# Graph network on one core: nodes numbered 49p+w, first edges found in a resident list

## What is computed

```
h = max(layernorm(x), 0)
x = x + GIN(GIN(h))        # GIN: h + segment_sum(h[src], dst), then two dense layers
h = max(layernorm(x), 0)
x = x + update(h, segment_sum(mlp(h)[src], dst))
```

## Time and profile before

| | |
|---|---|
| device time, median of 3 runs | 937.94 us (937.82 to 939.57) |
| span of the profiled execution | 976.2 us |
| `build` in it | 0 to 422 us |
| `net` in it | 422 to 976.2 us |

### The profile page before, as it was taken

One profiled execution on the slowest core, in us unless ns is written; L12 is line 12 of the kernel. 1 busy time (PEld: TensorE's weight loads), 2 busy tenths in 40 slices (PEclk: granted clock), 3 DMA queues, 4 the chain that ended last, 5 costly groups with the idle time before them and its releaser, 6 DMA issues.

```text
span 976.2 us, 25210 instructions
## 1 busy us (share of the span) xinstructions
PE 889.8 (91%) x11282; PEld 722.6 (74%) x11282; DVE 699.2 (72%) x656; ACT 479.9 (49%) x573; POOL 407.2 (42%) x281
## 2 busy tenths in 40 slices
PE   0577999859999999989999999999999999999996
PEld 0246988749999999967777777777777866777774
DVE  7784999829999999757456655555545686677773
ACT  2643645335544555346454554554555365555551
POOL 5874388870880000030663546760001143444450
PEclk9967999878999999999999999999999999999998
DMA  3022434414434334441444434444442367788871
GB/s 108 18 84 80 137 102 130 133 39 134 136 103 140 124 123 131 135 147 58 132 132 132 119 94 128 129 117 119 113 128 85 93 197 222 212 242 239 239 218 48
DMA packets 81857, 126.86 MB, mean 130 GB/s; under 512 B 10288, under 2 KB 58544, under 8 KB 81616
## 3 DMA queue, kind: packets, MB, share of 16 engines
q1 hardware_dynamic: 78608, 121.98, 41.7%
q0 software_dynamic: 3136, 3.22, 1.5%
HBM read 84.22 MB, written 40.94 MB: 128 GB/s over the span
## 4 chain that ended last, share of the span: by engine, by line
PE 49%; DVE 4%; ACT 2%; issue 1%; DMA 0%; POOL 0%; DVEq 0%; POOLq 0%; ACTq 0%
PE net_ps_hi L1271 14%; PE net_ps_lo L1271 14%; PE net_ps_hi L1288 7%; PE net_ps_lo L1288 6%; PE net_ps_mt L1214 4%; PE net_ps_ft L1214 2%; ACT net_wide L1110 1%; DVE net_wide L833 1%; PE net_ps_check L1306 1%; DVE hT L926 1%; DVE hT L921 1%; DVE net_first L933 1%; PE net_ps_mt L1318 0%; DMA net_raw<-edge_counts 0%; POOL net_wide L879 0%
## 5 line engine op out<-in xcount | busy, mean ns | idle before, releaser
L1271 PE MATMUL net_ps_hi<-net_wide,net_first 128*128 128x512 f32 (+1 forms) x637 | 248.5, 394 | 1.3 <-POOL net_wide L879 1.3
L338 DVE TENSOR_TENSOR build_hot_lo<-build_grid_lo,build_keys_t 128x4096 bf16<-128x4096 bf16 x100 | 225.3, 2284 | 26.7 <-PE build_ps_cnt L569 14.3
L1271 PE MATMUL net_ps_lo<-net_wide,net_first 128*128 128x512 f32 (+1 forms) x637 | 240.8, 382 | 0.0
L589 PE MATMUL build_ps_out<-build_parts_pad,build_cnts 128*128 128x195 bf16 x2401 | 234.9, 256 | 3.4 <-issue 1.9
L833 DVE CAST net_wide<-net_raw 128x3584 fp32r<-128x3584 uint8 (+1 forms) x90 | 201.2, 2243 | 44.2 <-PE net_ps_lo L1288 16.9
L1110 ACT ACTIVATE net_wide<-net_raw 128x3584 fp32r<-128x3584 uint8 (+1 forms) x64 | 193.6, 3025 | 78.9 <-PE net_ps_lo L1271 44.8
L456 ACT ACTIVATE build_cnts<-build_ps_cnt 128x980 uint16<-128x980 f32 (+3 forms) x176 | 150.5, 901 | 160.4 <-PE build_ps_cnt L569 130.5
L589 PEld LDWEIGHTS build_ps_out<-build_parts_pad,build_cnts 128*128 128x128 fp8e4 x2401 | 212.8, 101 | 11.3 <-issue 5.4
L259 POOL DMA_INDIRECT build_edges<-in_edges,build_start_i x49 | 114.6, 2339 | 70.2 <-DVE build_start_i L322 56.5
L1271 PEld LDWEIGHTS net_ps_hi<-net_wide,net_first 128*128 128x128 f32 x637 | 119.8, 188 | 31.9 <-issue 7.0
L1271 PEld LDWEIGHTS net_ps_lo<-net_wide,net_first 128*128 128x128 f32 x637 | 119.9, 188 | 24.7 <-issue 2.6
(11 more groups left out here) (171 smaller groups left out, 708.4 us busy)
## 6 DMA issues: line engine op xcount, KB each, us to landing
net_raw<-edge_counts SPq DMA_DIRECT2D x168, 448.0 KB, 3.7
edge_counts<-build_cnts SPq DMA_DIRECT2D x168, 224.0 KB
xres<-in_x SPq DMA_DIRECT2D x1, 1568.0 KB, 6.8
net_raw<-edge_counts SPq DMA_DIRECT2D x14, 112.0 KB, 2.0
out<-xres SPq DMA_DIRECT2D x12, 128.0 KB, 4.1
build_rows<-in_dst_rows,build_row_i POOLq DMA_INDIRECT x49
build_edges<-in_edges,build_start_i POOLq DMA_INDIRECT x49, 4.3
edge_counts<-build_cnts SPq DMA_DIRECT2D x7, 112.0 KB
```

What stands on the lines that cost most here:

```text
L338: return v.tensor_tensor(hot.rearrange("p c (k t) -> p c k t", t=2), grid[:, :].rearrange("p (k t) -> p k t", t=2)[:, None, :, :].broadcas ...
L589: last = nc.tensor.matmul(to, cnts[u % A_RING][:, w % 2, c, :], parts66[:, c, :, with_check], start=(c == 0), stop=False)
L1271: last = nc.tensor.matmul(ps[(b + 1) % 2][:, 0:n * P], first[:, c, lo:lo + H], expanded[e % WIDE_RING][:, 0:n, k, :], start=(c == 0), stop ...
```

## The change

Node n becomes lane n div 49, window n mod 49, so the 49 nodes of a lane are neighbours in the edge list. A list `listed` of every fourth destination around each lane's expected place (128 x 996 int16, made on the host with the inputs) is loaded first. ACT compares 600 of its entries with each window's node (`compare`), and the count gives the address of the run of edges within 4 edges, without histogram, row lookup or row gathers. Window and lane of a source are found by a multiplication by 1/49 and a rounding (5 DVE instructions for 4). x arrives in four shares, and the opening is reordered. From group 3 on each gather waits for a number of finished hot_lo tables.

```diff
+STARTS_AT = {3: (2, 0), 4: (3, 0), 5: (5, 0), 6: (7, 0), 7: (9, 0), 8: (11, 0)}
+FIRST_HOTS = {3: 8, 4: 12, 5: 20, 6: 28, 7: 43, 8: 59}
+HOTS_APART = {3: 1, 4: 2, 5: 1, 6: 2, 7: 2, 8: 2}
...
-                sp.dma_start(piv[:, :], a["piv"]).then_inc(piv_in, 16)
-                sp.dma_start(xin, a["x"].rearrange("p (w f) -> p w f", f=F)).then_inc(x_in, 16)
+                sp.dma_start(listed[:, :], a["listed"]).then_inc(listed_in, 16)
+                for q, w in enumerate(shares):
+                    sp.dma_start(xin[:, w, :], a["x"][:, w.start * F:w.stop * F].rearrange("p (w f) -> p w f", f=F)).then_inc(x_in[q], 16)
...
+                        if g in FIRST_HOTS:
+                            pool.wait_ge(hot_ready, FIRST_HOTS[g] + HOTS_APART[g] * (w - lo))
                         nc.gpsimd.indirect_dma_start(edges[:, w, :, :].rearrange("p e k -> p (e k)"), None, a["edges"],
...
-                    link(v.tensor_scalar(tile_no[:, 0:n, :], src, 7, None, ALU.logical_shift_right))
-                    v.scalar_tensor_tensor(keys[:, 0, lo:hi, :], tile_no[:, 0:n, :], float(-P), src, ALU.mult, ALU.add)
-                    link(v.scalar_tensor_tensor(scaled[:, 0:n, :], dst, 64.0, tile_no[:, 0:n, :], ALU.mult, ALU.add))
-                    v.tensor_tensor(keys[:, 1, lo:hi, :], scaled[:, 0:n, :],
+                    v.tensor_scalar(lane_f[:, 0:n, :], src, -float(NW // 2), 1.0 / NW, ALU.add, ALU.mult).then_inc(key_steps, 1)
+                    v.scalar_tensor_tensor(scaled[:, 0:n, :], dst, 64.0, src, ALU.mult, ALU.add).then_inc(key_steps, 1)
+                    dve.wait_ge(key_steps, 4 * g + 1)
+                    v.tensor_scalar(keys[:, 0, lo:hi, :], lane_f[:, 0:n, :], ROUNDER, -ROUNDER, ALU.add, ALU.add).then_inc(key_steps, 1)
+                    dve.wait_ge(key_steps, 4 * g + 3)
+                    v.scalar_tensor_tensor(lane_f[:, 0:n, :], keys[:, 0, lo:hi, :], -float(NW), scaled[:, 0:n, :], ALU.mult,
+                                           ALU.add).then_inc(key_steps, 1)
+                    dve.wait_ge(key_steps, 4 * g + 4)
+                    v.tensor_tensor(keys[:, 1, lo:hi, :], lane_f[:, 0:n, :],
...
+                    nc.scalar.activation(below[:, w % 2, :], listed[:, at:at + LOOK], ACT.Sign, bias=node2[:, w:w + 1], scale=-2.0,
+                                         accum_out=below_n[:, w:w + 1]).then_inc(compared, 1)
```

More of the change, by code:

```diff
@@ L142, in build @@
         small_b = sb("small_b", [P, P], BF16)
[L143 to L155, removed]
+        listed = sb("listed", [P, LISTED], I16)
+        below = sb("below", [P, 2, LOOK], BF16)
         below_n = sb("below_n", [P, NW])
@@ L179, in build @@
         links = ph.sem("vector_steps")
[L180 to L187, removed]
-        compared = ph.sem("rows_compared")
-        halves_ready = ph.sem("halves_ready")
+        key_steps = ph.sem("key_steps")
+        diagonal = ph.sem("diagonals_set")
+        listed_in = ph.sem("list_loaded")
+        x_in = [ph.sem(f"x_loaded{q}") for q in range(4)]
+        eps_set = ph.sem("eps_set")
+        compared = ph.sem("windows_compared")
         starts_known = ph.sem("starts_known")
@@ L275, in _ @@
                 for g in range(2, len(SPANS)):
-                    gather_edges(g, *SPANS[g])
-                    for later in ROWS_BEHIND.get(g, ()):
-                        gather_rows(later, *SPANS[later])
+                    gather_edges(g)
             @block.vector
@@ L526, in _ @@
                 round2(5)
+                copy_first(4, 6)
                 round1(6)
                 round2(6)
+                copy_first_keys(1)
+                copy_first_keys(2)
+                for w in range(10, OPENED):
+                    compare(w)
                 copy_first(6, steps(0))
                 for u in range(1, NU):
+                    later = compared_in(u)
                     for k in range(steps(u)):
@@ L534, in _ @@
                         copy_counts(u, k)
-                        for g in range(4, len(SPANS)):
-                            pair, at = compare_step(g)
-                            if u == pair and 0 <= k - at < STEP:
-                                compare_rows(g, 2 * (k - at), 2 * (k - at) + 2)
+                        for w in later[max(k - 1, 0):k] if len(later) <= 4 else later[k:k + 1]:
+                            compare(w)
             @block.tensor
@@ L595, in use @@
                             last.then_inc(summed_out, 1)
-                pe.wait_ge(piv_hot, 1)
-                for j in range(NPIV):
-                    last = nc.tensor.matmul(ps_hist, piv_lo[:, j, :], piv_hi[:, j, :], start=(j == 0), stop=(j == NPIV - 1))
-                last.then_inc(hist_out, 1)
-                pe.wait_ge(hist_ready, 1)
-                nc.tensor.matmul(ps_row, tri[:, :], hist[:, :], start=True, stop=False)
-                nc.tensor.matmul(ps_row, ones[:, :], hist_sum[:, :], start=False, stop=True).then_inc(ranked, 1)
-                pe.wait_ge(consts, 9)
+                pe.wait_ge(consts, 8)
+                pe.wait_ge(diagonal, 1)
                 turn_keys(0, first_keys[0]).then_inc(first_turned, 1)
```

211 lines of the change are left out of this document (93 added, 118 removed).

## The result

The changed kernel takes 943.43 us (943.34 to 946.37), the kernel before beside it 937.88 (937.23 to 939.57): ratio 1.0072, 95% interval 1.0054 to 1.0091. It is slower, where 931 and faster were forecast. Ratios are taken from the runs near each kernel's fastest alone, so they need not be the quotient of the medians.

The account below looks back on a forecast made before the run. DVE was taken to bound `build` outside its stalls, and PE `net`, left unchanged. Opening −5.8, edge wait −2.9 and keys +1.9 gave −6.8 us from the 937.94 median: 931.0 us, range 920 to 945.

Parts of the forecast that it names:

- the gates cost nothing: Gathers from group 3 on: by the lock rule one is held for one table at most, so 0 us.
- held gathers: Slower rival, groups 3 to 8: gated gathers stay until the next reduction, 36.5 us of waits, 967 us; chance 0.20.
- The sum: Whole kernel: −5.8 − 2.9 + 1.9 = −6.8 us, giving 931.0 us.
- the opening: Start of `build` to pair 2's first table of 6400: from 65.17 to 56.7 us.
- First keys: Opening: first keys at 16.3 us instead of 22.64, waiting for DVE and not for edges; gain 6.3 us.
- pair 1: Opening: pair 1's first table moves from 48.27 to 42.5 us, behind seven rounds on ACT and PE; −5.8 us.
- Keys: `find_keys` on DVE, five instructions for four: 2.39 to 2.73 us with eight windows, +1.9 us over groups 2 to 8.
- A comparison: ACT, 49 comparisons: 0.39 us becomes 0.71 each, hidden by DVE; zero in all, 2 us kept for the range.
- the two terms: Opening: pair 1's first table earlier, −5.8 us, and no wait for group 2's edges, −2.9 us.
- The rule: Shared DVE/GpSimd port lock lasts one instruction, so a gather is held one table at most; the sum stays 931.
- the 37.5 us: Seven DVE waits in the profile before, 65.1 to 408 us; timed runs taken to hardly have them.
- More gain: Faster rival: timed runs have part of the stalls, pacing removes 5 to 25 us, 905 to 926 us; chance 0.10.

Follow-up runs that it names:

- e1: Changed kernel with no gather gated by tables, nothing else changed: 936.69 us, ratio to the kernel before 1.0001.
- e2: Changed kernel with the gates of groups 7 and 8 one table later (44 and 60 for 43 and 59): 936.58 us, ratio 0.9989.
- e8: Kernel before once more, unchanged, for a second profile: 936.93 us, profiled span 935.3 us.
- e11: e5 with every comparison of 600 elements done twice on ACT, the first into a scratch tile: 936.89 us.
- e5: Changed kernel with gates 44 and 60, group 3's starts found right behind group 2's keys in pair 1, its gathers ungated: 929.54 us, ratio 0.9916.
- e16: e5 with group 8's seven gathers gated at 60, 64, 68, 70, 72, 74 and 76 finished hot_lo tables: 934.86 us.
- e6: Changed kernel, own gates, with a one-element memset behind each hot_lo table of pairs 2, 12, 13, 16, 17 and 18: 929.86 us, ratio 0.9921.
- e3: e2 with group 3's starts found in pair 1, after its third table, instead of pair 2, and its gathers ungated: 936.98 us.
- e13: e5 with only group 3's first gather ungated, the other three waiting for 9, 10 and 11 finished tables: 934.96 us.
- e15: Changed kernel once more, unchanged: 944.63 us, ratio 0.970 to the kernel before beside it.
- e17: e5 with group 8's seven gathers gated at 60, 63, 66, 68, 70, 72 and 74 finished hot_lo tables: 929.92 us.
- e9: e5 with no gates at all: 932.37 us.
- e14: Kernel before with 20 of its 49 row gathers issued once more into a scratch tile: 991.37 us against 969.6.
- e7: Changed kernel with the gates of e2 and a one-element memset behind the four tables of pair 2 alone: 930.57 us, ratio 0.9922.
- e10: e5 with the keys of pairs 1 and 2 turned and copied ahead of the seventh round's last two halves: 928.80 us.

## Why the prediction was wrong

**The step that failed** is the term put at nothing for the gathers: "the gates cost nothing" and, behind it, the chance of 0.20 for held gathers. It measured 14.3 us, in two parts. Groups 7 and 8 wait 4.97 and 2.37 us, and these waits are the gates': they go without gates (e1) and with gates one table later (e2). Group 3 waits 6.93 us, and 6.3 without any gate (e1): its first gather starts in the ninth table after the last `find_keys`, where before row gathers ran in between and none was held (e8). The sum had nothing for it, and the rival put it on the gate.

The rival had the mechanism and the sign; its price was put at 36.5 us, since I let half of all gathers be held and only seven were. For groups 3, 7 and 8 it came near (6.1, 4.8 and 3.6), groups 4 to 6 waited for nothing. The argument against it was that each gate opens at a table's end. That is no protection: the gather at 208.66 starts 0.36 us into a table just like the one at 195.97 that got in. What matters is the count of the last experiments. The gates of groups 7 and 8 have odd numbers, 43 and 59, so that every second gather opens beside a reduction, gets in there in 0.94 us (203.78) and does not restart the count; the next stands in the fifth table. With the even numbers of e2 each gets in between two tables, and the count stays at two or three. In a burst each gather let in starts the count again. The bursts before were not a flaw that pacing cures.

The reading of the earlier trace rows was also too mild. The trace of the kernel before has four held gathers, not two, and of the two edge gathers that began after a long pause of POOL both were held, not one:

```profile
114.43 10.55 POOL L259 DMA_INDIRECT build_edges<-in_edges,build_start_i  x1 [26.50 <-DVE build_start_i L322]
```

**The sum itself was right.** Of the opening I forecast −8.5 up to the first table of 6400; measured −9.9. First keys were forecast at 16.3 and stand at 17.0, pair 1 at 42.5 and 41.15. Keys were forecast at 2.73 us and took 2.73, +1.7 from group 3 on. A comparison took 0.79 us for 0.71 forecast, and they are hidden in the pairs (e11). Only the split of the opening is uncertain: I read it from the stalled execution, and against e8 (pair 1 at 44.74, a 6.2 us wait for group 2) the two terms are −3.6 and −6.2 for the −5.8 and −2.9 forecast. That their sum fits is partly luck. Without holds this gives 931.0 forecast and 929.5 measured (e5). With them: −9.8 + 1.7 + 14.3 = +6.2, and the tail, in which PE ends 2.0 us further behind DVE (12.9 for 10.9 us), gives +8.2. That is the difference between the starts of `net`, 390.71 and 382.48 in e8.

**The rule weighed against the trace.** The Trainium skill, "SBUF — State Buffer", section "Who interferes with whom", has the lock end with one instruction. The gathers of 1.90 to 3.95 us, which end with their table, agree with it. The held ones do not: the row at 268.76 of e16 stands across four tables, and a memset lets such a gather in (e6). I had named the row and the disagreement, and still let the rule lower the rival's chance. The measurement decides: the longest hold here stands across nine tables, 21.5 us in e3.

**The stalls.** I read the 37.5 us as belonging to the profiled execution, since the median matched without them. For the runs of that comparison this was right (e8: 935.3 without stalls). As a statement on the kernel it was wrong: in three of the six sets of runs the kernel before has them in its timed runs too, at 959 to 984 us. It is not the chip alone, for the record gives chip 3 for e5 to e8 (937.85) and for e13 to e15 (969.6). And it is not the kernel before alone: in these three sets the trace of every variant has "issue" gaps of PE in `build` from 60 us on, 1.9 to 5.5 us where there are no row gathers, and in the other three sets no trace has any but the first of the kernel before. Without row gathers no wait of DVE for PE goes with them, the tail apart.

"More gain" came true as a ratio only, at 3% for the change as it is and 4% for e17 (0.9591, 0.9520 to 0.9661), because the kernel before was slower there; no kernel reached its 905 to 926 us (931 less 25 is 906, not 905). It was not the pacing either: e9 has no gates and no such waits of DVE. That row gathers turn the gaps into 30 us is supported by e14 and not shown: no kernel without them differs from the kernel before in this alone. Why the gaps show in some sets of runs only is not known, and neither is what PE's sequencer lacks in them.

The best kernel is e5, with the starts of group 3 earlier and without their gate, and two gates one table later: 0.9916 of before where before does not stall. e6, e7, e10 and e17 are within its scatter.

## What to carry to other kernels

Before spacing out GpSimd gathers beside a VectorE that runs tensor_tensor without a break, look at how the isolated ones fare in the trace, not at the mean of the burst. Issue them within a few tables of the last gather let in or the last pause, not beside a reduction, or put a memset of one element where they must get in; it took 0.06 us here. When a rare row contradicts a rule and the change multiplies exactly that row's situation, the row deserves the larger chance. And when profile and median differ by a removable stall, run the kernel before again before deciding which of the two is typical.

## What was not expected of the hardware

A GpSimd gather beside VectorE tables gets in at the end of its table in the first to fourth table since `find_keys`, a pause or a gather let in between two tables. From the fifth on it waits until a reduction or a memset follows, 6.2 to 21.5 us here; a gather let in by the reduction does not restart the count, and the next behind it is held as well where DVE goes on with tables. This count was found in 17 traces and foretold two more; what in the chip counts is open. PE's instruction stream has gaps of 0.5 and 1.2 us between a few matmuls in some sets of runs and in others none. With the row gathers of the kernel before they go with a loss of 30 us, in the variants without them with none that shows in `build`.
